# First pair's weight operands stored to DRAM for the second pair, and seven-product down projection in the second pair's layer two

## The chip, the cores and the metric

The kernel runs on one core of a Trainium2 chip. The metric is the device time of one execution in microseconds, as the median of several runs. Engines: PE is TensorE (PEld its weight loads), DVE is VectorE, ACT is ScalarE, POOL is GpSimd, SP is SyncE, which issues all DMAs here.

## The reference, cut to what matters

Four sequences of 512 rows with 512 features go through an attention block with two feed-forward networks, and then through three adapter layers with experts picked for each sequence (the "units" of the kernel, 3 x 4 = 12).

```
attn_out = softmax(x Wq (x Wk)^T / sqrt(512)) (x Wv) Wp + bp
cms      = gelu(attn_out @ cW1 + cb1) @ cW2 + cb2 + one_hot(code)        # layer one:  512 -> 2048 -> 512
modifier = gelu(concat[attn_out, cms] @ mW1 + mb1) @ mW2 + mb2           # layer two: 1024 -> 2048 -> 512
y0       = clip(x + cms + modifier, 0, 1)
for layer in 1..3:   y = layernorm(y + gelu(y @ Wd[e] + bd[e]) @ Wu[e] + bu[e]) * gamma[e] + beta[e]
```

## The kernel before

**Arithmetic.** All data is 32 bit. Each operand of a product is split in a high part (a cast to fp32r, on ACT) and the rest (operand minus high part, on DVE). A product is three matmuls, high x high, high x low, low x high; `mm3` at line 557 issues them, so nearly all matmuls have that line.

**Feed-forward part.** The sequences go in two pairs. Each pair has 8 chunks: four of layer one, four of layer two (`chunk_of`; chunks 0 to 7 are the first pair, 8 to 15 the second). A chunk takes two hidden tile pairs ("quads", q = 0, 1). Its **up** part computes the hidden block of both row halves and both sequences with seven block products (P1, P6, P7, P5, P2, P4, P3) in place of eight, six matmuls of 128 x 512 for each part of a product: 14 steps in layer one, 28 in layer two (`up_quad`). P1's bank is copied to u_t by ACT (`copy_first`, line 930), and P2 goes on in the same bank; DVE combines the products (v_t, w_t, g), ACT does the gelu. A weight operand of a product is 128 x 256: raw pieces of 512 KB arrive in `rawp`, DVE makes four sums of blocks in `asum`, ACT casts an operand into one of six `ring` slots (`weight_hi`, line 906) and DVE subtracts (`weight_lo`, line 1224), AHEAD = 5 steps before its use. Both pairs do that with the same weights.

The **down** part has eight steps d of 12 matmuls (`down_chunk`), 96 in all: four row tiles by two sequences by four output tiles. It needs split rows of the down weight (`w_hl`, from `wraw`; `down_weight_hi`, `down_weight_lo` at line 1285) and splits of g (`g_hl`, three slots; `g_hi`, `g_lo`). During steps 0 to 4 ACT and DVE also make the first five ring operands of the next chunk. DVE adds the eight banks to `res` after it.

**SP's queue** is in order and written out by hand. At the start it loads the inputs, waits for the expert numbers and then runs 36 pieces of the adapter weights through three `prep` slots: load (line 419), cast on ACT (`piece_hi`), rest on POOL (`piece_lo`, line 1545), store (line 415). ACT has `piece_hi` between its copies out of PSUM and ahead of the exps (line 822). In the feed-forward part SP issues `raw_piece` (430), `down_weights` (435), seven 1 MB stores of the second pair's operands in chunks 1 to 3, their loads `next_a_operand` (441) in chunk 7, x of the first pair (`xs`, 2 MB) there, y0 of the first pair (`y0_spill`, 2 MB) in chunk 9 and its split (`y0_split`, 4 MB) in chunk 11. In the last chunk it loads yT, x of the second pair, y0, the first adapter weights (wd, wu), the up biases and twelve `unit_columns` of 5 KB (502).

**Hand-over to the adapters.** TensorE transposes y0 of sequence 0 (`y0_to_rows(0)`, line 721), does the down product of unit 0, transposes y0 of sequence 1, and goes on unit by unit. DVE first clips y0 of both sequences of the second pair (`second_pair_y0`, line 1362), then adds the bias to the rows (`y0_rows`, line 1442), and later sums z and takes its statistics (`z_stats`).

## Time and profile before

| | us |
|---|---|
| median of 3 runs | 1193.47 (1193.29 to 1194.72) |
| the profiled execution's own time | 1194.04 |
| its span in the trace | 1192.2 |
| PE busy | 1178.7 (99%) |
| DVE busy | 790.8 (66%) |
| ACT busy | 569.3 (48%) |
| POOL busy | 162.5 (14%) |
| DMA, mean busy share of 16 engines | 34.7%, 145.82 MB |

Busy times say how full an engine is. The chain that ended last says on which engine the time was spent that led to the end. In the timeline the bracket behind a row gives the idle time of the engine before it and who ended it. For DMAs two things count: when SP issues them, and when they land.

### The profile page before, as it was taken

The numbers are of one execution on the slowest core, as the hardware profiler recorded it, in microseconds if no ns is written. First come the engines' busy times: TensorE is split into PE (matmuls) and PEld (weight loads), VectorE is DVE, ScalarE is ACT, GpSimd is POOL, SyncE is SP. The second block draws the span as 40 slices with busy tenths as digits, with TensorE's granted clock in tenths as the row PEclk, the third lists the DMA queues.
The fourth block names the chain that finished last, engine by engine and source line by source line (L and its number), as shares of the span: only waits on it lengthen the run. The fifth ranks groups of instructions, "written<-read, shape, count | busy, mean of one in ns | idle before, by whom it ended". The sixth has DMA issues, their size and how long they took to land.

```text
span 1192.2 us, 15272 instructions
## 1 busy us (share of the span) xinstructions
PE 1178.7 (99%) x5328; PEld 973.9 (82%) x5328; DVE 790.8 (66%) x1460; ACT 569.3 (48%) x1068; POOL 162.5 (14%) x145
## 2 busy tenths in 40 slices
PE   9999999999999999999999999999999999999997
PEld 7888878888888788888888888878888888788886
DVE  6344486776678756565667686696656565877885
ACT  5434353563544534342435643554343434357886
POOL 1332230000000000000000000000000000349981
PEclk9999999999999999999999999999999999999999
DMA  6764452124320302020561321411111118746644
GB/s 226 273 216 161 164 175 94 54 60 153 124 96 28 107 13 95 10 98 8 194 258 53 124 62 45 178 53 53 54 53 54 54 36 326 223 142 224 218 167 169
DMA packets 50610, 145.82 MB, mean 122 GB/s; under 512 B 6356, under 2 KB 6356, under 8 KB 46310
## 3 DMA queue, kind: packets, MB, share of 16 engines
q1 hardware_dynamic: 50534, 144.84, 34.7%
q8 instruction: 43, 0.70, 0.2%
q14 instruction: 33, 0.27, 0.1%
HBM read 108.11 MB, written 36.71 MB: 121 GB/s over the span
## 4 chain that ended last, share of the span: by engine, by line
PE 92%; DVE 5%; issue 1%; DMA 1%; ACT 1%; POOL 0%; POOLq 0%; DVEq 0%; SPq 0%; ACTq 0%
PE psum L557 89%; PE psum L777 2%; DVE c_op L1334 1%; DVE res L1362 1%; DVE ring L1224 1%; DVE res L1307 1%; PE psum L608 0%; PE psum L591 0%; PE psum L721 0%; PE psum L604 0%; DMA wqk_raw<-wqk_dram 0%; DVE sm L1477 0%; DMA prep<-wdu_dram 0%; DVE z L1471 0%; DVE c_t L1319 0%
## 5 line engine op out<-in xcount | busy, mean ns | idle before, releaser
L557 PE MATMUL psum<-g_hl,w_hl 128*128 128x512 f32 x1536 | 351.3, 389 | 0.4 <-DVE w_hl L1285 0.4
L557 PEld LDWEIGHTS psum<-g_hl,w_hl 128*128 128x128 f32 x1536 | 288.1, 188 | 61.0 <-DVE w_hl L1285 0.8
L557 PE MATMUL psum<-a_op,ring 128*128 128x512 f32 x1344 | 316.7, 389 | 0.7 <-DVE w_t L1266 0.7
L557 PEld LDWEIGHTS psum<-a_op,ring 128*128 128x128 f32 x1344 | 252.1, 188 | 54.0 <-DVE w_t L1266 1.5
L906 ACT CAST ring<-asum 128x256 fp32r<-128x256 f32 x192 | 77.2, 404 | 210.5 <-PE psum L557 160.0
L557 PE MATMUL psum<-c_op,ring 128*128 128x512 f32 x672 | 163.9, 391 | 0.8 <-DVE c_op L1334 0.6
L557 PEld LDWEIGHTS psum<-c_op,ring 128*128 128x128 f32 x672 | 125.5, 188 | 29.4 <-DVE c_op L1334 3.6
L1292 DVE TENSOR_TENSOR g_hl<-g,g_hl 128x512 fp32r<-128x512 f32 x128 | 88.2, 689 | 67.9 <-ACT g_hl L946 66.5
L1553 POOL TENSOR_TENSOR yT<-res,yT 128x512 fp32r<-128x512 f32 x8 | 11.7, 1488 | 846.3 <-ACT yT L1044 846.3
L1224 DVE TENSOR_TENSOR ring<-asum,ring 128x256 fp32r<-128x256 f32 x192 | 80.5, 421 | 56.1 <-ACT ring L906 54.9
L946 ACT CAST g_hl<-g 128x512 fp32r<-128x512 f32 x128 | 78.3, 618 | 77.5 <-PE psum L557 77.5
L923 ACT ACTIVATE g<-g,sm 128x512 f32<-128x512 f32 x96 | 69.5, 724 | 78.8 <-DVE g L1272 31.5
L1224 DVE TENSOR_TENSOR ring<-rawp,ring 128x256 fp32r<-128x256 f32 x144 | 60.7, 423 | 62.8 <-ACT ring L906 61.6
L906 ACT CAST ring<-rawp 128x256 fp32r<-128x256 f32 x144 | 57.6, 404 | 55.3 <-PE psum L557 55.3
L1307 DVE TENSOR_TENSOR res<-psum,res 128x512 f32<-128x512 f32 x96 | 64.8, 691 | 20.2 <-PE psum L557 18.6
L557 PE MATMUL psum<-wu,h_hl 128*128 128x512 f32 x288 | 68.4, 393 | 0.0
L557 PE MATMUL psum<-yT,wd 128*128 128x512 f32 x288 | 67.8, 391 | 0.0
L1545 POOL TENSOR_TENSOR prep<-prep 128x512 f32<-128x512 f32 x36 | 50.2, 1401 | 126.4 <-ACT prep L817 126.4
L557 PEld LDWEIGHTS psum<-yT,wd 128*128 128x128 f32 x288 | 53.8, 188 | 11.1
L557 PEld LDWEIGHTS psum<-wu,h_hl 128*128 128x128 f32 x288 | 53.3, 188 | 10.7
L1285 DVE TENSOR_TENSOR w_hl<-wraw,w_hl 128x512 fp32r<-128x512 f32 x64 | 44.1, 689 | 20.3 <-ACT w_hl L937 19.3
L557 PE MATMUL psum<-vp_w,xT 128*128 128x512 f32 x192 | 45.3, 391 | 0.0
(128 smaller groups left out, 1352.7 us busy)
## 6 DMA issues: line engine op xcount, KB each, us to landing
rawp<-up_w_dram SPq DMA_DIRECT2D x48, 512.0 KB, 3.6
wdu_split<-prep SPq DMA_DIRECT2D x36, 512.0 KB, 2.9
wraw<-dn_w_dram SPq DMA_DIRECT2D x64, 256.0 KB, 3.3
wd<-wdu_split SPq DMA_DIRECT2D x12, 1024.0 KB, 9.1
wu<-wdu_split SPq DMA_DIRECT2D x12, 1024.0 KB, 5.4
prep<-wdu_dram SPq DMA_DIRECT2D x36, 256.0 KB, 3.3
second_pair_operands<-c_op SPq DMA_DIRECT2D x7, 1024.0 KB, 6.3
a_op<-second_pair_operands SPq DMA_DIRECT2D x7, 1024.0 KB, 11.7
```

The source lines that it names most:

```text
L557: ins = nc.tensor.matmul(ps, lw(el), rw(er), start=first and i == 0, stop=last and i == 2, skip_group_check=skip)
L777: ins = nc.tensor.transpose(tr_bank(u, d)[:, i * P:(i + 1) * P], z[u % 3][:, i, d * P:(d + 1) * P], ident[:, :])
L906: nc.scalar.copy(ring[n % RING][:, 0, :], aop_src(n)).then_inc(aop_hi, 1)
L923: nc.scalar.activation(dst, src, ACT.Gelu, bias=(cb1, mb1)[l][:, t:t + 1]).then_inc(gelu_done, 1)
L946: nc.scalar.copy(g_hl[t % GHL][:, 0, :], g[:, q, 2 * row + seq, :]).then_inc(g_hi_done, 1)
L1224: nc.vector.tensor_tensor(ring[n % RING][:, 1, :], aop_src(n), f(ring[n % RING][:, 0, :]), ALU.subtract).then_inc(aop_lo, 1)
L1285: nc.vector.tensor_tensor(w_hl[t % 2][:, 1, :], wraw[t % 2][:, :], f(w_hl[t % 2][:, 0, :]), ALU.subtract).then_inc(w_lo_done, 1)
L1292: nc.vector.tensor_tensor(g_hl[t % GHL][:, 1, :], g[:, q, 2 * row + seq, :], f(g_hl[t % GHL][:, 0, :]), ALU.subtract).then_inc(g_lo_done, 1)
L1307: nc.vector.tensor_tensor(dst, bank[4 * seq + m], dst, ALU.add).then_inc(d_evac, 1)
L1334: nc.vector.tensor_tensor(c_ops[i][:, 1, :, :], src, f(c_ops[i][:, 0, :, :]), ALU.subtract).then_inc(op_lo[2 + p], 1)
L1362: nc.vector.tensor_scalar(res[:, 2 + seq, m, :], res[:, 2 + seq, m, :], 0.0, 1.0, ALU.max, ALU.min).then_inc(y0_done, 1)
L1545: nc.gpsimd.tensor_tensor(prep[i][:, 1, :], prep[i][:, 1, :], prep[i][:, 0, :], ALU.subtract).then_inc(p_lo, 1)
```

## The change

The first pair stores each finished ring operand (high and low part, 256 KB) to DRAM (`store_operand`), 168 of them. The second pair doesn't split up weights: SP loads each operand into its ring slot as soon as the operand six steps earlier is used (`load_operand`). In layer one of the second pair (chunks 8 to 11), ACT and DVE use the freed time to split 56 operands of the layer-two down weight into four `stage` slots, from where they are stored too; the cast for slot n waits for the store of n - 4. In layer two of the second pair (chunks 12 to 15), the down part uses seven block products: 14 steps of six matmuls, with 14 splits of g or of sums of g (`g_sum`, `g_op_hi`, `g_op_lo`) and seven adds of two banks (`down_product_add`). The transfers of x, y0 and y0_split are cut into pieces of 512 KB and put between the ring loads of chunks 8, 9 and 10. The twelve `unit_columns` go to the start, ahead of the prep pieces. In the last chunk and behind it the loads are put between and behind the ring loads, and DVE adds x and clips after `y0_rows(0)` and `y0_rows(1)`.

```diff
+CS = NCHUNK + NCHUNK // 2
+LOADED = AOP
+PREPARED = AOP + PROD * QL
+DOWN_STEPS = (tuple((i, 0) for i in (P1, P6, P7, P5)) + tuple((i, 1) for i in (P1, P6, P7, P5))
+              + tuple((i, q) for i in (P2, P4, P3) for q in range(QC)))
+CSTEP = len(DOWN_STEPS)
+STG = 4
+DG = 8
...
+            for u in range(LAYERS * B):
+                unit_columns(u)
+
             def bsum_store():
...
+            def store_operand(n):
+
+                sp.wait_ge(aop_lo, n + 1)
+                src = f(aop_dst(n)[:, :, :].rearrange("p e n -> p (e n)"))
+                if n < LOADED:
+                    sp.dma_start(up_ops[n], src).then_inc(s_wst[n % RING], 16)
+                else:
+                    sp.dma_start(down_ops[n - LOADED], src).then_inc(s_dst[n % STG], 16)
+
+            def load_operand(r):
+                sp.wait_ge(aop_used, r - RING + 1)
...
+                sp.dma_start(f(ring[r % RING][:, :, :].rearrange("p e n -> p (e n)")),
+                             (up_ops, down_ops)[down][i]).then_inc(s_ring[r % RING], 16)
...
+            for r in range(LOADED, LOADED + RING):
+                load_operand(r)
+            for i in (P2, P4, P3):
+                next_a_operand(NCHUNK - 1, i)
...
+            for ci in range(NCHUNK, CS):
+                first, ops = aop_at(ci, 0), QC * PROD
+                down_weights(4 * ci)
+                down_weights(4 * ci + 1)
+                for k in range(-STG, ops):
+                    if k >= 0:
+                        load_operand(first + RING + k)
+                    if k + STG < ops:
+                        store_operand(first + STG + k)
+                        pieces_after(first + STG + k)
+                    if ci == NCHUNK and 4 <= k < 8:
+                        x_piece(k - 4)
+                    if ci == NCHUNK + 1 and 0 <= k < 4:
+                        y0_piece(k)
+                    if ci == NCHUNK + 2 and 1 <= k < 9:
+                        y0_split_piece(k - 1)
+                    if k == ops - 3:
+                        down_weights(4 * ci + 2)
+                down_weights(4 * ci + 3)
...
+            last_up = aop_at(NCH - 1, 1)
+            for r in range(PREPARED + RING, TOTAL):
+                load_operand(r)
+                if r in (last_up + RING + 3, last_up + RING + 5):
+                    split_rows(0, (r - last_up - RING - 3) // 2)
+                if r == last_up + RING + 7:
+                    unit_down(0)
+                if r in (last_up + RING + 13, last_up + RING + 15):
+                    seq = (r - last_up - RING - 13) // 2
+                    sp.wait_ge(aop_used, last_up + LAYER_STEPS[1].index((P3, 0)) + 1)
+                    sp.dma_start(xs[1][:, seq, :, :], xin[2 + seq]).then_inc(s_xs[1], 16)
+                if r == last_up + RING + 16:
+                    for b in range(B):
+                        sp.dma_start(bup0[:, b, :], bup_all[bass.ds(ex[b], 1)].to_broadcast([P, V])).then_inc(t_bup0, 16)
+            sp.wait_ge(s_spill, 16 * 4)
+            sp.wait_ge(aop_used, dop_at(NCH - 1, 7) + 1)
             sp.dma_start(res[:, 0, :, :], y0_dram[:, 0]).then_inc(s_y0in[0], 16)
...
             unit_up(0)
+            unit_down(1)
+            for e in range(2):
+                split_rows(1, e)
+            sp.wait_ge(aop_used, dop_at(NCH - 1, 8) + 1)
+            sp.wait_ge(f_done, 3)
             sp.dma_start(res[:, 1, :, :], y0_dram[:, 1]).then_inc(s_y0in[1], 16)
-            unit_down(1)
             unit_up(1)
...
+            def down_products(ci):
+                for step, (prod, q) in enumerate(DOWN_STEPS):
+                    r, t = dop_at(ci, step), CSTEP * (ci - CS) + step
+                    if q == 0:
+                        down_step_bank_free(ci, prod)
+                    pe.wait_ge(s_ring[r % RING], 16 * ((r - LOADED) // RING + 1))
+                    pe.wait_ge(dg_lo, t + 1)
+                    for m in range(2):
+                        ins = mm3(bank[ADD_BANK[ADDS.index(prod)] + m], lambda e: ring[r % RING][:, e, m * P:(m + 1) * P],
+                                  lambda e: dg[t % DG][:, e, :], prod <= P5 and q == 0, q == QC - 1, skip=prod > P5)
+                    ins.then_inc(aop_used, 1)
...
-                nc.scalar.copy(ring[n % RING][:, 0, :], aop_src(n)).then_inc(aop_hi, 1)
+                if n < LOADED:
+                    if n >= RING:
+                        act.wait_ge(aop_used, n - RING + 1)
+                        act.wait_ge(s_wst[n % RING], 16 * (n // RING))
+                elif n < LOADED + STG:
+                    act.wait_ge(aop_used, LOADED)
+                else:
+                    act.wait_ge(s_dst[n % STG], 16 * ((n - LOADED) // STG))
+                nc.scalar.copy(aop_dst(n)[:, 0, :], aop_src(n)).then_inc(aop_hi, 1)
...
-            second_pair_y0(0)
-            second_pair_y0(1)
+            down_product_add(NCH - 1, 6)
             y0_rows(0)
...
                 if s == 0:
+                    x_add(0)
+                    second_pair_y0(0)
                     h_lo(0, 0)
                     h_lo(0, 1)
                     y0_rows(1)
+                    x_add(1)
+                    second_pair_y0(1)
```

## Rows read from the trace of the kernel before

**Rows 1.** The page, busy times and the chain that ended last.
```profile
PE 1178.7 (99%) x5328; PEld 973.9 (82%) x5328; DVE 790.8 (66%) x1460; ACT 569.3 (48%) x1068; POOL 162.5 (14%) x145
...
PE 92%; DVE 5%; issue 1%; DMA 1%; ACT 1%; POOL 0%; POOLq 0%; DVEq 0%; SPq 0%; ACTq 0%
```

**Rows 2.** Timeline of PE (start, duration, us), down 7, up 8, down 8.
```profile
594.40 21.92 PE L557 MATMUL psum<-g_hl,w_hl 128*128 128x512 f32 x96
616.16 19.20 PE L557 MATMUL psum<-a_op,ring 128*128 128x512 f32 x84
635.20 21.92 PE L557 MATMUL psum<-g_hl,w_hl 128*128 128x512 f32 x96
```

**Rows 3.** Timeline of PE, chunk 12: up begins, one gap, down begins.
```profile
779.36 5.60 PE L557 MATMUL psum<-a_op,ring 128*128 128x512 f32 x24
...
792.34 1.67 PE L557 MATMUL psum<-c_op,ring 128*128 128x512 f32 x6 [0.28 <-DVE c_op L1334]
...
819.41 21.92 PE L557 MATMUL psum<-g_hl,w_hl 128*128 128x512 f32 x96
```

**Rows 4.** Line 502, two column loads; duration ns, first and last start us.
```profile
L502 SPq DMA_DIRECT2D unit_columns<-pp_dram x2: 332/332/333, 1014.6 to 1015.2; - x2
```

**Rows 5.** Timelines of SP, ACT and POOL in the first phase of pieces.
```profile
18.70 0.83 SPq L419 DMA_DIRECT2D prep<-wdu_dram  x2
...
26.61 0.44 SPq L419 DMA_DIRECT2D prep<-wdu_dram  x1
...
21.98 0.62 ACT L817 CAST prep<-prep 128x512 fp32r<-128x512 f32 x1
...
30.91 1.29 POOL L1545 TENSOR_TENSOR prep<-prep 128x512 f32<-128x512 f32 x1 [3.94 <-ACT prep L817]
...
47.08 0.62 ACT L817 CAST prep<-prep 128x512 fp32r<-128x512 f32 x1 [2.11 <-DMA prep<-wdu_dram]
47.60 0.68 ACT L822 ACTIVATE probs<-psum,sm 128x512 f32<-128x512 f32 x1
```

**Rows 6.** Timelines of PE and DVE, attention of the first sequence.
```profile
49.95 8.33 PE L557 MATMUL psum<-vp_w,xT 128*128 128x512 f32 x36
...
62.63 10.72 PE L557 MATMUL psum<-pT,v_n 128*128 128x512 f32 x46
...
63.91 0.68 DVE L1109 TENSOR_TENSOR v_n<-psum,v_n 128x512 fp32r<-128x512 f32 x1
```

**Rows 7.** Windows: us, busy of PE, PEld, DVE, ACT, POOL, PEclk, DMA share, GB/s.
```profile
585.00:590.00 5.00, 5.00 (x24) 4.14 (x23) 3.77 (x7) 1.82 (x4) 0.00 (x0) 1.00 0.96 333
600.00:605.00 5.00, 5.00 (x23) 4.14 (x23) 3.00 (x6) 2.38 (x5) 0.00 (x0) 1.00 1.02 426
1058.00:1062.00 4.00, 4.00 (x21) 3.30 (x19) 3.99 (x10) 0.69 (x1) 2.25 (x3) 1.00 1.05 404
```

**Rows 8.** A lone 256 KB load (line 435, at 630.1); 256 KB stores at the end.
```profile
DMA to landing us min/median/max: 2.5/2.5/2.5
...
out_dram<-res SPq DMA_DIRECT2D x8, 256.0 KB, 2.2
```

**Rows 9.** Groups of instructions: busy us, mean ns, idle before.
```profile
L906 ACT CAST ring<-asum 128x256 fp32r<-128x256 f32 x192 | 77.2, 404 | 210.5 <-PE psum L557 160.0 <-DVE asum L1239 48.6 <-DVE asum L1242 2.0
...
L930 ACT COPY u_t<-psum 128x512 f32<-128x512 f32 x32 | 18.7, 586 | 0.0
...
L1357 DVE TENSOR_TENSOR res<-res,xs 128x2048 f32<-128x2048 f32 x2 | 4.6, 2289 | 1.1 <-DMA xs<-x_dram 1.1
```

**Rows 10.** Timeline of SP in chunk 7.
```profile
585.61 2.07 SPq L441 DMA_DIRECT2D a_op<-second_pair_operands  x4
```

**Rows 11.** Timeline of DVE, down part of chunk 7, last down weight.
```profile
606.79 0.69 DVE L1285 TENSOR_TENSOR w_hl<-wraw,w_hl 128x512 fp32r<-128x512 f32 x1
```

**Rows 12.** Timeline of PE, transposes of y0 of sequences 0 and 1.
```profile
1020.70 1.91 PE L721 MATMUL psum<-ident,res 128*128 128x128 f32 x16
...
1029.41 2.36 PE L721 MATMUL psum<-ident,res 128*128 128x128 f32 x16 [1.32 <-DVE res L1442]
```

More of the change, by code:

```diff
@@ L1022, in _ @@
                                 g_hi(ci, {1: 0, 2: 1, 4: 2}[at_])
+                if ci >= CS:
+                    gelu(ci, 1, C12)
+                    for d in range(CSTEP):
+                        for step in G_OP_DOWN.get(d, ()):
+                            g_op_hi(ci, step)
+                    continue
                 for d in range(DSTEP):
@@ L1095, in _ @@
                 if s == 0:
+                    y0_hi(2)
                     y0_hi(3)
@@ L1404, in _ @@
                                 g_lo(ci, {1: 0, 2: 1, 4: 2}[at_])
+                if ci >= CS:
+                    combine_12(ci, 1)
+                    for d in range(CSTEP):
+                        for k in G_SUM_DOWN.get(d, ()):
+                            g_sum(ci, *k)
+                        if d in ADD_AT:
+                            down_product_add(ci, ADD_AT[d])
+                        for step in G_OP_DOWN.get(d, ()):
+                            g_op_lo(ci, step)
+                        if ci == NCH - 1 and d in (9, 11, 13):
+                            first_sum_add((9, 11, 13).index(d))
+                    continue
                 for d in range(DSTEP):
```

308 lines of the change are left out of this document (230 added, 78 removed).

## The prediction

> **What bounds the kernel now.** I read the page first. Its busy times and the chain that ended last [rows 1] say the same: TensorE is busy for 1178.7 of 1192.2 us and carries 92% of the chain. So a matmul that goes away is worth its full time, and every wait that TensorE gets is paid in full. Next I read TensorE's timeline. A chunk of the feed-forward part is 84 matmuls up and 96 down in layer one, back to back: 616.16 to 635.20 is 19.04 us, and 594.40 to 616.16 is 21.76 us [rows 2]. Both give 0.2267 us for each matmul. One up product of six matmuls is a step of 1.36 us. The only gaps in the feed-forward part of the second pair stand at the start of its layer two, where the operands of that layer come late from DVE [rows 3].
>
> The second thing to read is the DMA queue. All DMAs are issued by SP in order, and they run through one hardware queue. Before the change that queue is mostly idle in the second pair, and the change fills it.
>
> **What the change removes.** In chunks 12 to 15 the down part goes from 96 to 84 matmuls: 4 x 12 x 0.2267 = **-10.9 us**. In the same chunks DVE and ACT no longer split weights. Up part 12 lasts 819.41 - 779.36 = 40.05 us, and its 168 matmuls would be 38.08 us, so 1.97 us is stall, waiting for c_op on DVE [rows 3]. DVE's queue there holds the weight work between the c_op jobs. When it goes, the c_op jobs move up, by more than the 0.3 us gaps: **-1.9 us** (between -1.97 and 0). The 14 operand splits per chunk that come instead of 8 are spread over a DVE that has lost its weight work. I walked its queue through one down part (sums, splits, PSUM adds at about 0.69 us each) and each product finds its operand about 1 us early or more; I cost this at nothing, and at 1 us per chunk if that cover fails.
>
> **Columns at the start.** The twelve loads of unit_columns move from the last chunk, where they cost TensorE nothing, to a place ahead of the prep pieces in SP's queue. At an idle queue they are issued 0.55 us apart: two of them start at 1014.6 and 1015.2 [rows 4]. (Behind a full queue, earlier in that series, they took up to twice that; I take the row of the idle queue, since at 18.7 us little is in flight.) So the first prep load goes from 18.70 to 18.7 + 12 x 0.55 = 25.3 us. It lands 3.3 us later, as it does now (18.70 to 21.98), at 28.6. The cast takes 0.62, POOL 1.3, and then SP stores it and issues the third load, at 31.0 instead of 26.61 [rows 5]: 4.4 us late. From there on the pieces have no slack. ACT waits for the DMA before the last piece at 47.08 as well [rows 5], and ACT has the pieces ahead of the exps. So the first exp ends at 52.7 instead of 48.3 [rows 5]. TensorE wants its bank at 49.95 and waits 2.8 us [rows 6]. In the next round a piece stands ahead of the pT and v_n copies: the last v_n half ends at 64.59, and the k = 3 matmul of the product that began at 62.63 wants it at 62.63 + 9 x 0.227 = 64.67 [rows 6]. That leaves 0.1 us, so nearly the whole 4.4 us arrives: **+4.3 us**. Bounds: 2.5 us if an issue costs 0.4 us, the cost of a prep load's issue, and 9 us if it costs 0.94.
>
> **Staging in the second pair's layer one.** I count in units of 256 KB. Saturated, the queue moved 426 GB/s with 8 KB rows and 404 with 2 KB rows [rows 7]; I take 415, which is 0.63 us for a unit. One unit alone lands in 2.5 us as a load and in 2.2 us as a store [rows 8], so a load has 1.9 us and a store 1.6 us on top of its transfer. In each step SP issues the load for the operand six products on, and the store of the stage operand four on; stage operand j+4 can't be cast before the store of operand j has landed, and ACT is blocked there with copy_first and the gelus queued behind it. Two units per 1.36 us step is 1.26 us: it just fits. What is put between them doesn't.
> - Chunk 10, y0_split as eight pieces of 2 units. From the end of product 0 until the load of operand 13 lands: 8 loads + 7 stores + 6 pieces x 2 + a raw piece of 2 = 29 units, 18.3 + 1.9 = 20.2 us. TensorE wants it after 12 x 1.36 = 16.3 us. Stall 3.9 us.
> - Chunk 9, y0 as four pieces. Until store 9: 6 + 6 + 8 + 2 = 22 units, 13.9 + 1.6 = 15.5 us, then the cast and copy_first behind it, 0.40 + 0.59 [rows 9]: 16.5 us. The P2 product of the second quad wants u_t after 13.6 us. Stall 2.9 us.
> - Chunk 8, x as four pieces: 23 units until load 13, 14.5 + 1.9 = 16.4 against 16.3 us. Stall 0.1 us.
> - Down part of chunk 7. The next-pair operands are issued from about 587.5 on (now 585.61 [rows 10]; the last stores of layer two come first). Then 28 units of a_op, three of down weights, six ring loads and the first stage store, 38 x 0.63 = 23.9 us, plus 1.0 for the first stretch, which ran at 333 GB/s [rows 7], plus 1.6: 614.0 us. That store is behind down weight 33, which waits for w_lo at 607.48 [rows 11], so issue isn't the limit. ACT is blocked on it with g_hi(7) behind: 0.40 + 0.62 + 0.69 gives 615.7 us, and step 7 begins at 594.40 + 7 x 2.72 = 613.4. Stall 2.3 us.
>
> Sum **+9.2 us**. Bounds: 3 us, if each of the four waits is met by 1.5 us of slack that I don't see; 13 us if the rate is 404 GB/s and each wait meets another 0.6 us.
>
> In the first pair one unit per step is stored (the queue is less than half full), each store is issued some five steps before its slot is wanted, and I cost it at nothing. If SP were blocked there in front of a store, ACT would feel it; the DMA waits that it passes (down weights, pieces) are all satisfied by then.
>
> **Chunk 15 and the end.** The queue there gets yT, wd, x and up-bias loads among the ring loads. Counted from the start of the down part, the load behind x and the four biases needs 5 + 8 + 4 = 17 units, 10.7 + 0.3 left over + 1.9 = 12.9 us, and it is wanted after 9 x 1.36 = 12.2: **+0.7 us** (0 to 2). Then res[:, 1], y0 of the second sequence, is now the last of 45 units: 28.4 + 0.3 + 1.9 = 30.6 us. The transposes of y0_to_rows(1) want it 19.04 + 0.7 + (1029.41 - 1.32 - 1020.70 = 7.39) = 27.1 us after the same point [rows 12]. That is 3.5 us of wait where 1.32 us of another wait (DVE clips before y0_rows) is now: **+2.2 us** (-1.3 to 4.5). DVE now does x_add(1), 2.3 us [rows 9], and four clips between y0_rows(1) and z_stats(0), in which the next transposes wait for z: **+0.8 us** (0 to 3).
>
> **The sum** is -10.9 - 1.9 + 4.3 + 9.2 + 0.7 + 2.2 + 0.8 = +4.4 us. It is made against the profiled execution, 1194.04 us (1.8 us around its span), which lies 0.6 us above the median of 1193.47. So 1198.4 on the profile's scale, **1197.9 us** as a median.
>
> **A rule weighed.** The stretch at 600 us moved 426 GB/s from DRAM into SBUF for 5 us, with the DMA engines' share at 1.0 [rows 7]. The Trainium skill, "DMA: Bandwidth & Descriptors", section "Specifications", gives about 358 GB/s as the HBM limit of a core, and the same page says that this side binds for transfers between HBM and SBUF. By 358 a unit would be 0.73 us, and the same counts would add about 3 us in chunk 10, 2 each in chunks 8 and 9, 4 in chunk 7 and 5 at the end: an estimate of some 1214 us. The trace disagrees for loads; no row has loads and stores mixed at saturation.
>
> **Rivals.**
> - *The queue is hidden.* The staging waits don't reach TensorE, because SP itself is held back (stores wait for aop_lo) and ACT's jobs have more room than I give them. For: the ring is six deep, and ACT isn't the engine that bounds the kernel now. Against: the byte counts leave nothing in chunk 10. Then -10.9 - 1.9 + 4.3 + 0.7 + 2.2 + 0.8 = -4.8: 1188.7 us, and 1187 with the cheap start. It decides the sign: faster as soon as staging costs under 4.8 us. Chance 0.27.
> - *Half of it.* The start costs 2.5 us and the staging about 5 us: -10.9 - 1.9 + 2.5 + 5 + 3.7 = -1.6, 1191.9 us, and with what lies around it (1191.1 to 1195.9) no change that can be told. Chance 0.15.
> - *The mixed queue is slow.* Loads and stores together run at the 333 GB/s that the stretch at 585 us had with a share of 0.96 [rows 7]: 0.79 us a unit. Then chunk 10 costs 8.5, chunk 9 6.4, chunk 8 3.8 and chunk 7 7.4 us, and the wait at the end is 10.7 us: about 1222 us. The page of the rule above is on this side. Chance 0.08.
> - *The products don't fit the down part.* DVE adds seven pairs of banks and makes 14 splits; if they come 1 us late in each of four chunks, 1202 us. In the range of my forecast.
>
> **How the numbers follow.** My forecast, slower by 2.4 to 12 us, has 0.50. A measurement of this kernel can tell about 0.2% (2.4 us) from no change. Faster 0.27, same 0.15, slower 0.50 + 0.08 = 0.58. The range leaves out about one in ten at each end: below the cheapest version of the hidden queue (1187) and above my upper bounds taken together for start and staging without the slow mixed queue (1208). My forecast's own range is 1196 to 1206.
>
> **What would show it.** In the profile of the changed kernel the twelve column loads stand before the first prep load, which goes out near 25 us; TensorE has a wait on ACT or DVE near 50 us and one near 65 us. Eight pieces of y0_split put a wait for the DMA of ring in the up part of chunk 10, some 4 us; chunks 8 to 10 last longer than 40.8 us, chunks 12 to 15 last 57.1 us. TensorE's transposes near the end wait for the DMA of res. If chunks 8 to 10 last 40.8 us, the queue count is wrong, and the kernel is faster.

## The result, and the profile after

The changed kernel takes **1237.2 us** (median of 4 runs, 1234.7 to 1239.8) against 1194.1 in the same session, a ratio of 1.036 with the interval 1.0335 to 1.0384: slower by some 43 us. I had forecast 1197.9 with a range from 1187 to 1208. The sign was right, the size was not. The profiled execution took 1237.19 us and has a span of 1235.4, 43.2 us more than before. Here are the lines of its page that answer to [rows 1]:

```profile
span 1235.4 us, 15542 instructions
...
PE 1185.1 (96%) x5280; PEld 972.4 (79%) x5280; DVE 761.7 (62%) x1351; ACT 531.2 (43%) x964; POOL 162.6 (13%) x146
...
PE 77%; DMA 9%; DVE 7%; SPq 2%; ACT 2%; issue 2%; POOL 1%; POOLq 0%; DVEq 0%; ACTq 0%
PE psum L710 75%; DMA down_operands<-stage 4%; DMA prep<-wdu_dram 2%; PE psum L970 2%; DMA ring<-down_operands 1%; DMA experts<-experts_dram 1%; DVE g_hl L1521 1%; POOL prep L1851 1%; DMA res<-y_spill 1%; DVE c_op L1561 1%; DVE a_op L1376 0%; SPq L481 0%; ACT prep L1010 0%; PE psum L744 0%; DVE xs L1568 0%
```

Two things stand in these lines. TensorE has 48 matmuls fewer and is still busy for 6.4 us longer. By count it should be busy for 1178.7 - 10.9 = 1167.8 us, so its matmuls ran 17.3 us slower. And its idle time has gone from 13.5 to 50.3 us. The chain, once TensorE with a rest, now goes through stage stores (4%) and g_hl. The waits of TensorE say who ended that idle time (us in total, times, longest):

```profile
PE psum L710 <- DVE g_hl L1521: 12.6, 3, 5.9
PE psum L710 <- DMA ring<-up_operands: 7.8, 7, 1.9
PE psum L710 <- DMA ring<-down_operands: 5.8, 2, 4.6
PE psum L710 <- ACT u_t L1132: 5.2, 3, 2.5
...
PE psum L710 <- ACT probs L1015: 3.0, 1, 3.0
```

TensorE's timeline (start, duration, [idle before <- releaser]) has them in place. These are waits of chunks 7 to 10, then the start of chunk 15, its two longest waits and the first transposes behind it:

```profile
599.97 19.20 PE L710 MATMUL psum<-g_hl,w_hl 128*128 128x512 f32 x84
625.07 5.18 PE L710 MATMUL psum<-g_hl,w_hl 128*128 128x512 f32 x12 [5.89 <-DVE g_hl L1521]
...
674.37 4.49 PE L710 MATMUL psum<-g_hl,w_hl 128*128 128x512 f32 x12 [2.38 <-DVE g_hl L1521]
...
697.18 2.18 PE L710 MATMUL psum<-a_op,ring 128*128 128x512 f32 x6 [1.89 <-DMA ring<-up_operands]
...
730.01 5.49 PE L710 MATMUL psum<-g_hl,w_hl 128*128 128x512 f32 x12 [4.30 <-DVE g_hl L1521]
...
756.88 1.65 PE L710 MATMUL psum<-a_op,ring 128*128 128x512 f32 x6 [2.49 <-ACT u_t L1132]
...
996.25 5.60 PE L710 MATMUL psum<-a_op,ring 128*128 128x512 f32 x24
...
1036.51 12.51 PE L710 MATMUL psum<-dg,ring 128*128 128x512 f32 x54 [1.19 <-DMA ring<-down_operands]
1053.64 9.99 PE L710 MATMUL psum<-dg,ring 128*128 128x512 f32 x30 [4.63 <-DMA ring<-down_operands]
1063.47 1.91 PE L914 MATMUL psum<-ident,res 128*128 128x128 f32 x16
```

Look at the durations too. The 12 matmuls at 625.07 took 5.0 us until the next part began, where 12 x 0.2267 is 2.7. The windows (us, busy of PE, PEld, DVE, ACT, POOL, PEclk, DMA share, GB/s) show why:

```profile
625.00:630.00 5.00, 4.93 (x12) 3.97 (x13) 4.38 (x8) 0.01 (x1) 0.00 (x0) 0.53 0.01 2
635.00:640.00 5.00, 5.00 (x24) 4.14 (x23) 1.95 (x5) 0.81 (x2) 0.00 (x0) 1.00 0.92 288
...
730.00:735.00 5.00, 4.99 (x12) 3.93 (x13) 4.33 (x7) 0.00 (x0) 0.00 (x0) 0.50 0.00 0
...
1045.00:1050.00 5.00, 4.01 (x18) 3.00 (x16) 5.00 (x9) 0.62 (x1) 0.00 (x0) 1.00 0.95 201
1055.00:1060.00 5.00, 5.00 (x13) 3.84 (x12) 2.42 (x3) 0.00 (x0) 0.00 (x0) 0.52 1.02 406
```

Behind the waits of 5.9, 4.3 and 4.6 us the granted clock is 0.50 to 0.53, the lower of TensorE's two levels (1.2 GHz). So such a wait costs more than its length.

From the starts of the parts in this timeline the whole difference can be laid out, against 0.2267 us for a matmul. The start is 216.26 against 210.65 us before. Chunk 15 is 67.2 us from 996.25 to 1063.47, where its 252 matmuls are 57.1. The row behind it is the stretch from the end of the last down part to the last of the transposes of y0, 38.05 us from 1063.47 against 36.86 from 1020.70 [rows 12], and the last one is all that follows, 133.9 us against 134.6:

| part | forecast | measured |
|---|---|---|
| start, up to the first a_op matmul | +4.3 | +5.6 |
| chunk 7, down (30.1 us for 21.8) | +2.3 | +8.4 |
| chunk 8, up / down (22.5 / 26.1) | +0.1 / 0 | +3.5 / +4.3 |
| chunk 9, up / down (27.8 / 28.8) | +2.9 / 0 | +8.8 / +7.0 |
| chunk 10, up / down (26.9 / 21.8) | +3.9 / 0 | +7.9 / 0 |
| chunk 11, up | 0 | +0.1 |
| chunk 12's stalls | -1.9 | -2.0 |
| 48 matmuls | -10.9 | -10.9 |
| chunk 15 | +0.7 | +10.1 |
| rows and first units behind it | +3.0 | +1.2 |
| the rest of the adapters | 0 | -0.8 |
| sum | +4.4 | +43.2 |

### The profile page after: what moved, and what is told of

Its sections match the earlier page's. It is cut to its first block, busy times and chain, and to the rows that moved or that the text cites. A ratio compares the mean times of both kernels' runs of the same rounds, so it can differ in the third digit from the quotient of the medians.

```text
span 1235.4 us, 15542 instructions
## 1 busy us (share of the span) xinstructions
PE 1185.1 (96%) x5280; PEld 972.4 (79%) x5280; DVE 761.7 (62%) x1351; ACT 531.2 (43%) x964; POOL 162.6 (13%) x146
## 4 chain that ended last, share of the span: by engine, by line
PE 77%; DMA 9%; DVE 7%; SPq 2%; ACT 2%; issue 2%; POOL 1%; POOLq 0%; DVEq 0%; ACTq 0%
PE psum L710 75%; DMA down_operands<-stage 4%; DMA prep<-wdu_dram 2%; PE psum L970 2%; DMA ring<-down_operands 1%; DMA experts<-experts_dram 1%; DVE g_hl L1521 1%; POOL prep L1851 1%; DMA res<-y_spill 1%; DVE c_op L1561 1%; DVE a_op L1376 0%; SPq L481 0%; ACT prep L1010 0%; PE psum L744 0%; DVE xs L1568 0%
## 5 line engine op out<-in xcount | busy, mean ns | idle before, releaser
L710 PE MATMUL psum<-g_hl,w_hl 128*128 128x512 f32 x1152 | 270.8, 396 | 13.0 <-DVE g_hl L1521 12.6
L710 PEld LDWEIGHTS psum<-g_hl,w_hl 128*128 128x128 f32 x1152 | 220.1, 192 | 61.4 <-DVE g_hl L1521 13.8
L710 PEld LDWEIGHTS psum<-c_op,ring 128*128 128x128 f32 x672 | 125.8, 188 | 27.8 <-DVE c_op L1561 1.8
L1521 DVE TENSOR_TENSOR g_hl<-g,g_hl 128x512 fp32r<-128x512 f32 x96 | 66.1, 688 | 49.5 <-ACT g_hl L1148 48.4
L710 PE MATMUL psum<-dg,ring 128*128 128x512 f32 x336 | 80.1, 400 | 5.8 <-DMA ring<-down_operands 5.8
L1105 ACT CAST ring<-asum 128x256 fp32r<-128x256 f32 x96 | 38.5, 404 | 104.1 <-PE psum L710 76.0
L710 PEld LDWEIGHTS psum<-dg,ring 128*128 128x128 f32 x336 | 65.0, 194 | 20.4 <-DMA ring<-down_operands 5.1
L1148 ACT CAST g_hl<-g 128x512 fp32r<-128x512 f32 x96 | 58.4, 617 | 45.0 <-PE psum L710 45.0
L1132 ACT COPY u_t<-psum 128x512 f32<-128x512 f32 x32 | 18.7, 584 | 88.8 <-PE psum L710 88.7
L1453 DVE TENSOR_TENSOR ring<-asum,ring 128x256 fp32r<-128x256 f32 x96 | 40.1, 420 | 26.4 <-ACT ring L1105 25.8
L1534 DVE TENSOR_TENSOR res<-psum,res 128x512 f32<-128x512 f32 x72 | 47.4, 687 | 13.1 <-PE psum L710 13.0
L1453 DVE TENSOR_TENSOR ring<-rawp,ring 128x256 fp32r<-128x256 f32 x72 | 30.3, 422 | 32.0 <-ACT ring L1105 31.4
```

The lines of the kernel that those rows point to most:

```text
L710: ins = nc.tensor.matmul(ps, lw(el), rw(er), start=first and i == 0, stop=last and i == 2, skip_group_check=skip)
L1105: nc.scalar.copy(aop_dst(n)[:, 0, :], aop_src(n)).then_inc(aop_hi, 1)
L1132: nc.scalar.copy(u_t[:, :], bank[4 * q + BANK_OF[P1]]).then_inc(u_done, 1)
L1148: nc.scalar.copy(g_hl[t % GHL][:, 0, :], g[:, q, 2 * row + seq, :]).then_inc(g_hi_done, 1)
L1453: nc.vector.tensor_tensor(aop_dst(n)[:, 1, :], aop_src(n), f(aop_dst(n)[:, 0, :]), ALU.subtract).then_inc(aop_lo, 1)
L1521: nc.vector.tensor_tensor(g_hl[t % GHL][:, 1, :], g[:, q, 2 * row + seq, :], f(g_hl[t % GHL][:, 0, :]), ALU.subtract).then_inc(g_lo_done, 1)
```

## Why the down parts stall

The g_hl waits, in parts that I had costed at nothing apart from chunk 7's, are the largest of TensorE's waits in total, 12.6 us. Down part 8 begins at 652.62. Rows of DVE, SP and ACT in it:

```profile
657.75 0.43 DVE L1453 TENSOR_TENSOR stage<-rawp,stage 128x256 fp32r<-128x256 f32 x1 [0.42 <-ACT stage L1105]
...
663.51 5.41 SPq L543 DMA_DIRECT2D wraw<-dn_w_dram  x2
668.96 2.05 SPq L526 DMA_DIRECT2D down_operands<-stage  x4
...
672.25 0.40 ACT L1105 CAST stage<-rawp 128x256 fp32r<-128x256 f32 x1 [7.35 <-DMA down_operands<-stage]
672.56 0.61 ACT L1148 CAST g_hl<-g 128x512 fp32r<-128x512 f32 x1
```

The first stage operand is complete at 658.2. SP stores it at 668.96, since the two down weights stand ahead of it in SP's order, and the second waits for DVE's last w_lo. The store lands 3.2 us later. ACT then makes the fifth staged operand, whose slot this was, and only then g_hl(7), whose buffer TensorE had freed at 652.62 + 5 x 2.72 = 666.2. There are four stage slots, and ACT and DVE work five products ahead. That is my theory of the down parts, **the order**: a cast one place too far ahead couples TensorE to a store that is issued late. The rival is **the queue**: the stores land late because the queue is full, whatever the order. In chunk 7 the queue has a case. The stage stores went out at 613.46 behind 28 units of a_op, and ACT was released at 623.36. In chunk 10 the same cast waits too:

```profile
779.02 0.41 ACT L1105 CAST stage<-rawp 128x256 fp32r<-128x256 f32 x1 [4.55 <-DMA down_operands<-stage]
```

There the last w_lo is done 13.1 us after the part's start (15.9 and 14.8 us in chunks 8 and 9), and g_hl(7) is ready 0.6 us before TensorE wants it. So it is a near miss, not a part without the chain.

## The experiments

The bracket is a 95% interval of the ratio.

| kernel | us | against the kernel before |
|---|---|---|
| the change | 1237.2 | 1.036 (1.0335 to 1.0384) |
| column loads late | 1229.0 | 1.0303 (1.0281 to 1.0326) |
| g_hi first | 1224.6 | 1.0261 (1.0240 to 1.0282) |
| one less ahead | 1216.2 | 1.0173 (1.0156 to 1.0191) |
| stage stores first | 1217.8 | 1.0189 (1.0167 to 1.0210) |
| and pieces moved | 1206.7 | 1.0111 (1.0094 to 1.0128) |
| and columns, up bias moved | 1201.0 | 1.0057 (1.0036 to 1.0078) |
| and store ahead of load | 1197.5 | 1.0021 (1.0008 to 1.0034) |
| and a lighter end | 1195.0 | 1.0003 (0.9993 to 1.0012) |
| and one less ahead, end in order | 1189.0 | 0.9957 (0.9943 to 0.9970) |
| before, 48 matmuls fewer | 1182.9 | 0.9908 (0.9891 to 0.9924) |

**The columns, put back behind the prep pieces.**

```diff
-            for u in range(LAYERS * B):
-                unit_columns(u)
-
             def bsum_store():
...
+            for u in range(LAYERS * B):
+                unit_columns(u)
             sp.wait_ge(op_lo[0], PROD)
```

> The changed kernel with one thing put back: the twelve unit_columns loads are issued behind the 72 prep loads and 72 stores instead of ahead of them. Theory (the start term is right in kind): TensorE's feed-forward part begins 5.6 us earlier, at 210.7 instead of 216.3 us, the V product begins at 49.95 instead of 52.90, and the whole is 5.6 us faster, 1231.6 us. Rival (the start's delay comes from elsewhere, or is taken up later by another wait): less than 2 us. Nothing else in the trace should move but by a shift.

1229.0 us. The gain by the medians is 8.2 us, of which 5.2 can be seen in the trace as the start; the intervals don't separate it from 5.6. (The prep loads and stores that the expectation counts as 72 each are 36 each.) The executions of these stalled kernels lie 4 to 7 us apart, so small steps between them are read from the places in the trace and not from the medians. The rows of the changed kernel, SP's and then TensorE's, followed by TensorE's first a_op row of this experiment:

```profile
18.93 7.13 SPq L481 DMA_DIRECT2D unit_columns<-pp_dram  x12
26.11 0.91 SPq L505 DMA_DIRECT2D prep<-wdu_dram  x2
...
52.90 10.04 PE L710 MATMUL psum<-vp_w,xT 128*128 128x512 f32 x36 [2.98 <-ACT probs L1015]
...
67.47 11.53 PE L710 MATMUL psum<-pT,v_n 128*128 128x512 f32 x48
...
216.26 6.05 PE L710 MATMUL psum<-a_op,ring 128*128 128x512 f32 x26
```

```profile
211.02 11.27 PE L709 MATMUL psum<-a_op,ring 128*128 128x512 f32 x49
```

The g_hl waits stayed in their places and nearly in their length (5.15, 2.50 and 3.86 us for 5.89, 2.38 and 4.30), so the start's delay is one of its own.

**g_hl(7) ahead of the fifth staged operand.** The same edit is made on DVE.

```diff
-                    if d < AHEAD and ci + 1 < CS:
+                    late = ci + 1 >= NCHUNK
+                    if d < AHEAD - late and ci + 1 < CS:
                         weight_hi(aop_at(ci + 1, 0) + d)
+                    if late and d == AHEAD and ci + 1 < CS:
+                        weight_hi(aop_at(ci + 1, 0) + AHEAD - 1)
```

> The changed kernel, but in the down parts of chunks 7 to 10 ACT and DVE do the split of the next chunk's fifth staged weight operand behind the split of g_hl(7) instead of ahead of it; SP's order is untouched. Theory (TensorE waits for g_hl(7) because ACT is held at that operand's cast until a stage store has landed, and g_hi(7) is queued behind): the waits on DVE g_hl before the eighth block of chunks 7, 8 and 9 (5.89, 2.38 and 4.30 us) go, and with each the slow stretch behind it; chunk 7's down part goes from 30.1 to about 22 us, chunk 8's from 26.1 to 22, chunk 9's from 28.8 to 22: 15 to 19 us less, about 1219 us. Rival (the next up part then waits for the late operand's own store instead, so the wait is only moved): the down parts are 21.8 us, but the up parts of chunks 8 to 10 grow by what is gained, and the whole is within 4 us of 1237.

1224.6 us: 12.6 less, between theory and rival. All three g_hl waits are gone, but the place behind them has its own. TensorE's rows in up part 8:

```profile
624.09 7.10 PE L710 MATMUL psum<-a_op,ring 128*128 128x512 f32 x30 [2.57 <-DVE res L1537]
...
642.40 1.66 PE L710 MATMUL psum<-a_op,ring 128*128 128x512 f32 x6 [2.35 <-ACT u_t L1132]
```

DVE is now held at the fifth operand with down_add (L1537) queued behind it, which empties the banks for the next part. So it isn't enough to take g_hl out from behind the blocked cast, since whatever comes behind it then is blocked in its place.

**Stage stores first.**

```diff
-                down_weights(4 * ci)
-                down_weights(4 * ci + 1)
-                for k in range(-STG, ops):
+                for k in range(STG):
+                    store_operand(first + k)
+                    if k % 2:
+                        down_weights(4 * ci + k // 2)
+                if ci == NCHUNK:
+                    for i in (P2, P4, P3):
+                        next_a_operand(NCHUNK - 1, i)
+                for k in range(ops):
```

> The changed kernel, but SP issues the first four stage stores of chunks 8 to 11 between the down weights (store, store, weight, store, store, weight) instead of behind both weights, and ahead of the loads of a_op P2, P4 and P3 in chunk 7. Theory (the stores are late because they are issued late, at 16.3 us into the down part of chunk 8): they are issued up to 6 us earlier, land before ACT wants the slot, and the waits on g_hl in the down parts of chunks 7 to 9 go: 15 to 19 us less, about 1219 us, nearly the same gain as from changing the order on ACT. Rival (the queue itself is full, and a store issued earlier lands no earlier): chunk 7 keeps its 5.9 us wait and chunk 9 its 4.3; the gain is under 5 us, from chunk 8 alone.

1217.8 us, 19.4 less, as the theory has it. The g_hl waits of chunks 7, 8 and 9 are all gone, and chunk 7's down part runs without a gap:

```profile
600.49 21.92 PE L712 MATMUL psum<-g_hl,w_hl 128*128 128x512 f32 x96
622.25 15.12 PE L712 MATMUL psum<-a_op,ring 128*128 128x512 f32 x66
```

In the changed kernel the queue was nearly idle before the stores of chunks 8 and 9 (a DMA share of 0.09 from 660 to 665 us and of 0.14 from 715 to 721), so the order on SP alone held them back. In chunk 7 the edit also takes 12 units of a_op from ahead of the stores. Order and queue aren't separated there.

**One number: four ahead instead of five.** SP's order is left as it was.

```diff
+def ahead(ci):
+
+    return AHEAD if ci < NCHUNK else AHEAD - 1
...
-                    if d < AHEAD and ci + 1 < CS:
+                    if d < ahead(ci + 1) and ci + 1 < CS:
                         weight_hi(aop_at(ci + 1, 0) + d)
```

> The changed kernel with one number changed: in chunks 8 to 11 ACT and DVE make a staged weight operand four products ahead of its place instead of five (there are four stage slots). SP's order is that of the changed kernel. Theory (five ahead with four slots is what couples TensorE to the landing of a store: operand j+4's cast waits for store j while g_hi and copy_first stand behind it): no cast in a down part has to wait for a stage store, so the g_hl waits of chunks 7, 8 and 9 go with their slow stretches (19.6 us over the nominal 21.8 us of these parts), and the u_t waits of the up parts shrink as well: 20 to 25 us less, 1212 to 1217 us. Rival (the slot's wait only moves to the first products of the next up part, as it did when the split of g_hl was put ahead): 10 to 13 us less, 1224 to 1227.

1216.2 us, 21 less. ACT's rows and then TensorE's, for chunk 7:

```profile
615.33 0.62 ACT L1153 CAST g_hl<-g 128x512 fp32r<-128x512 f32 x1 [1.58 <-PE psum L715]
624.38 0.41 ACT L1110 CAST stage<-rawp 128x256 fp32r<-128x256 f32 x1 [8.44 <-DMA down_operands<-stage]
...
601.47 21.92 PE L715 MATMUL psum<-g_hl,w_hl 128*128 128x512 f32 x96
623.23 15.12 PE L715 MATMUL psum<-a_op,ring 128*128 128x512 f32 x66
```

The store lands as late as in the changed kernel, at 624.4, and no one is waiting: g_hl(7) is made at 615.3, when TensorE frees its buffer. This decides for the order. The late store is harmless until something that TensorE needs is queued behind it. The u_t waits went too, but 10.3 us of waits on ring<-up_operands stayed in up parts, and 4.0 us on w_t.

**The one-time pieces out of the up parts**, on top of stage stores first.

```diff
-                    if ci == NCHUNK and 4 <= k < 8:
-                        x_piece(k - 4)
-                    if ci == NCHUNK + 1 and 0 <= k < 4:
-                        y0_piece(k)
-                    if ci == NCHUNK + 2 and 1 <= k < 9:
-                        y0_split_piece(k - 1)
...
+                if ci == NCHUNK:
+                    for k in range(4):
+                        x_piece(k)
+                if ci == NCHUNK + 3:
+                    for k in range(8):
+                        y0_split_piece(k)
```

> The stores-first kernel, and in it the one-time traffic of the second pair's layer one is taken out of the up parts: the x pieces go out at the start of chunk 8's down part, the y0 pieces after the first stage stores of chunk 10, the eight y0_split pieces at the start of chunk 11's down part, and the a_op loads P1, P6, P7, P5 inside chunk 7's store loop; DVE's y0_add jobs move to steps 2 to 5 of chunk 8's down part. Theory (the up parts of chunks 8, 9 and 10 stall because these pieces stand between ring loads and stage stores that have 1.36 us each): the waits on u_t and ring there (2.2, 6.0 and 5.6 us, with the half-clock stretches behind them some 20 us) go, up parts of 19.1 us as in chunk 11, and the whole is about 1199 us. Rival (a store takes so long to land, 3 to 5 us, that ACT is held whatever stands between): the u_t waits stay in chunks 8 to 10, the gain is under 8 us, above 1210 us.

1206.7 us: 11.1 less, where I expected 19. The waits on ring<-up_operands in chunks 8 to 10 are all gone, so the pieces were their cause. Waits of 0.5 to 1.1 us on u_t and 0.8 on w_t stayed, 5.2 us with all of them, so a part of the rival was true. In the two profiled executions the up parts of chunks 8 to 11 lose 15.5 us (22.6 us above 19.04 each before, 7.1 after), more than the 11.1 of the medians; the rest of the difference isn't explained.

**Columns late and the up bias spread out**, on top of that.

```diff
-                if r == last_up + RING + 16:
-                    for b in range(B):
+                if r - last_up - RING in (8, 9, 10, 11):
+                    for b in (r - last_up - RING - 8,):
```

> The pieces-moved kernel with two more edits: the column loads behind the prep pieces, and the four up-bias loads of the last chunk one by one among ring loads 8 to 11 of the last quad instead of together behind load 16. Theory: the start gives back 5.6 us, and the wait of 4.6 us on ring with its slow stretch in the last down part shrinks to under 1.5 us, together some 10 us: 1189 us, below the kernel before. Rival (the bytes of the last chunk don't fit wherever they stand): the same wait shows up earlier, in the last up part or on yT at its end, and only the 5.6 us of the start are gained, 1193.5 us.

1201.0 us, 5.8 less: the start, and nothing from chunk 15. Its waits of 1.2 and 4.5 us on ring became three of 1.2, 1.3 and 1.8, and the wait on res behind it grew from 1.6 to 3.6 us. The rival held in this, though the wait went behind the chunk and not ahead of it: with this order and these bytes, what is moved off one load lands on another.

**Each store ahead of its step's load**, on top of that (chunks 8 to 11).

```diff
                 for k in range(ops):
-                    load_operand(first + RING + k)
                     if k + STG < ops:
                         store_operand(first + STG + k)
+                    load_operand(first + RING + k)
+                    if k + STG < ops:
                         pieces_after(first + STG + k)
```

> The all-moved kernel, and in chunks 8 to 11 each step issues its stage store ahead of its ring load instead of behind it. Theory (what is left in those up parts, waits of 0.6 to 0.9 us on u_t and of 0.8 us on w_t, 5.6 us in all, comes from stores that SP holds back behind a load that waits for TensorE, so that ACT's cast and copy_first behind it come a step late): a store goes out up to 1.36 us earlier, those waits go, and the kernel takes 5 us less, 1196 us. Rival (a store is issued as soon as DVE has made it anyway, and the rest is the landing of 3 to 4 us): the waits stay as they are, under 1 us of gain.

1197.5 us, 3.5 less. The u_t waits are gone, the three on w_t of 0.6 to 0.8 us stayed.

**A lighter end**, on top of that. In the code DG goes from 8 to 6, and x_add is called in chunks 13 and 14.

```diff
+                if ci == 4:
+                    for b in range(B):
+                        sp.dma_start(bup_rows[:, b, :], bup_all[bass.ds(ex[b], 1)].to_broadcast([P, V])).then_inc(s_bupd, 16)
...
+                if r == last_up + RING + 9:
+                    sp.wait_ge(s_bupd, 16 * B)
+                    sp.dma_start(bup0[:, :, :], bup_rows).then_inc(t_bup0, 16)
```

> The store-ahead kernel with less traffic in chunk 15: the four one-row up-bias loads are made once into DRAM rows in chunk 4 (DRAM to DRAM) and read at the end as one load of 4 units; x of the second pair comes in four pieces in chunks 12 to 14 and is added there by DVE, through two buffers for which the ring of down-part operands dg shrinks from eight to six. Theory (the last chunk loses 4.2 us of waits on ring and 3.6 on res, with slow stretches, because its queue holds some 10 to 12 us more than fits): 8 units of x and 4 us of the one-row loads less (9 us of queue) take those waits to under 2 us together: 8 to 10 us faster than the store-ahead kernel, about 1187 us, below the kernel before (1194). Rivals: six dg buffers are too few and TensorE waits on dg in each of the four down parts (1 us each or more); or the one-row reads weren't the cause and the waits stay, 1194 us.

1195.0 us, 2.4 less where I expected 8 to 10 (the two intervals overlap a little). No wait on dg appeared, so six buffers do. The ring waits of the last down part shrank to 2.0 us, but the wait for res grew:

```profile
PE psum L930 <- DMA res<-y_spill: 5.5, 1, 5.5
```

SP issues that load last, behind one wu, one wd and two yT loads, when DVE's last sum is done. The queue was a third idle from 1005 to 1015 us (a share of 0.69 and 0.61) and full from 1015 on.

**The end in the order of need**, and four ahead, on top of that.

```diff
+                if r in (last_up + RING + 19, last_up + RING + 21):
+                    split_rows(1, (r - last_up - RING - 19) // 2)
-                if r == last_up + RING + 9:
+                if r == last_up + RING + 16:
...
-            unit_up(0)
             unit_down(1)
-            for e in range(2):
-                split_rows(1, e)
+            unit_up(0)
```

> The lighter-end kernel with that same four-ahead rule, and with chunk 15's loads in the order of their need: yT of the second sequence among the last ring loads, the up-bias rows at ring load 16, and res[1] right behind one wd and one wu load instead of behind those and two yT loads. Theory (the 5.5 us wait on res<-y_spill in the lighter-end kernel is 8 units of yT ahead of it in a full queue, while the queue was a quarter to a third idle from 1000 to 1015 us): that wait goes to under 1 us, and the 0.8 us waits on w_t in chunks 8 to 10 go too: 6 to 8 us less than 1195.0, about 1188 us, below the kernel before (1194.0) by 0.5%. Rival (bytes moved earlier make the ring loads late by as much): waits on ring in the last down part grow by 3 us or more, and it stays within 0.2% of the kernel before.

**1189.0 us** (1188.4 to 1190.2), 6.0 less and 0.4% below the kernel before. The 5.5 us wait shrank to 0.5, but the load of y0 of sequence 0 now comes 2.6 us late; the w_t waits are gone. The main waits of TensorE in it that the kernel before doesn't have:

```profile
PE psum L935 <- DMA res<-y_spill: 3.1, 2, 2.6
...
PE psum L731 <- DMA ring<-up_operands: 1.6, 2, 1.1
...
PE psum L731 <- DMA ring<-down_operands: 1.2, 1, 1.2
PE psum L731 <- DVE g_hl L1542: 0.9, 1, 0.9
```

What it gains is 5.1 of the 12.8 us that the idea is worth (10.9 of matmuls, 1.9 of chunk 12's stalls); most of the rest is in these rows.

**What the matmuls are worth**, on the kernel before. It leaves out one of the three terms in steps 1, 3 and 5 of the last four down parts.

```diff
+                            short=ci >= 3 * NCHUNK // 2 and d in (1, 3, 5)).then_inc(d_used, 1)
```

> The kernel before with 12 of the 96 matmuls left out of the down parts of chunks 12 to 15 (one of the three terms of steps 1, 3 and 5 is not computed), nothing else changed. Theory (what the products remove is worth its full time, 48 x 0.2267 us): 10.9 us faster, 1183.0 us. Rival (DVE's or ACT's splits become what TensorE waits for once the down part is 19 us long): new waits on g_hl or w_hl in chunks 12 to 15 and a gain under 6 us.

1182.9 us, 11.6 less (9 to 13 by the interval), and no wait on g_hl or w_hl that wasn't there before. The term of 10.9 us was right.

**TensorE's clock behind a wait**, on the kernel before.

```diff
+                    if q == 1 and pos == 0 and ci in PROBES:
+                        pe.wait_ge(s_probe, sorted(PROBES).index(ci) + 1)
```

> The kernel before, with eight waits put into TensorE's order, one ahead of the second quad of chunks 0, 1, 2, 3, 8, 9, 10 and 11, each ended by GpSimd after 1, 3, 6, 9, 13, 18, 26 and 40 small fills (idle of about 0.5 to 8 us). Theory (an idle of some 2 us or more costs its own length and then 4 to 5 us at half clock, about 2.3 us more): the chunks with a wait under 1 us are longer by the wait alone, those with a wait over 2 us by the wait and 2 to 2.5 us, with a granted clock near 0.5 for a few us behind it. Rival (the slow stretches in the changed kernel come from something else, the DMA traffic or the matmuls' own operands): each chunk is longer by exactly its wait, and the granted clock stays at 1.0 behind all eight.

Eight waits of 0.47 to 6.57 us, each followed by the 42 matmuls of a quad. Four of them:

```profile
633.31 9.80 PE L560 MATMUL psum<-a_op,ring 128*128 128x512 f32 x42 [2.35 <-POOL sm L1564]
...
677.52 12.64 PE L560 MATMUL psum<-a_op,ring 128*128 128x512 f32 x42 [3.13 <-POOL sm L1564]
...
725.82 12.37 PE L560 MATMUL psum<-a_op,ring 128*128 128x512 f32 x42 [4.38 <-POOL sm L1564]
...
776.04 11.23 PE L560 MATMUL psum<-a_op,ring 128*128 128x512 f32 x42 [6.57 <-POOL sm L1564]
```

Behind the waits up to 2.35 us the quad takes 9.80 us (9.68 without a wait). Behind those of 3.13, 4.38 and 6.57 us it takes 2.8, 2.6 and 1.4 us more. The granted clock is 0.50 just behind all three; it is still 0.74 from 682 to 685 us behind the first, and at 1.00 from 780 us on behind the last. So the slow stretches do come from waiting, and the longest wait didn't cost most. The Trainium skill, "TensorE: Matmul & The Clock Gate", section "HAM oscillation — how this bites in real kernels", tells of the same with DMA waits, behind each of which the matmuls start at the slower clock. The trace agrees, with the 0.50 behind these three. In the changed kernel the waits of 2.38 us at 674.37 and of 2.98 at 52.90 had slow stretches behind them as well (1.6 and 1.7 us), so the length of one wait doesn't settle it.

**The queue alone**, behind the last output of the kernel before.

```diff
+            for group in ((load,), (store,), (load, store), (rows_of_one,), (store, load)):
+                for i in range(8):
+                    for job in group:
+                        job(i)
+                sp.wait_ge(s_b, moved[0])
```

> The kernel before, and behind its last output store the chip only moves 256 KB units of 2 KB rows, each group waited for: 8 loads; 8 stores; 8 loads and 8 stores alternating; 8 loads that give one DRAM row to all 128 partitions; 8 and 8 again, store first; one load, one store, one of the one-row loads. Theory of the prediction: 0.63 us a unit in every group (loads 5 + 1.9 us, stores 5 + 1.6, mixed 10.1 + 1.9), a lone load 2.5 and a lone store 2.2 us. Rival that the changed kernel suggests: a unit of the mixed group takes 0.73 to 0.8 us (13 to 15 us for 16), a lone store over 3 us, and a one-row load 1.2 us (9.6 + 2 us for 8), since the stretch of the up-bias loads moved 201 GB/s.

SP's rows. Each group starts when the one before it has landed, so the starts give the times:

```profile
1191.27 3.67 SPq L554 DMA_DIRECT2D res<-dn_w_dram  x8
1200.12 4.46 SPq L558 DMA_DIRECT2D traffic<-res  x8
1206.94 0.33 SPq L554 DMA_DIRECT2D res<-dn_w_dram  x1
...
1220.15 6.58 SPq L562 DMA_DIRECT2D res<-bup_dram  x8
1234.94 0.33 SPq L558 DMA_DIRECT2D traffic<-res  x1
...
1250.02 0.33 SPq L558 DMA_DIRECT2D traffic<-res  x1
1252.03 0.34 SPq L562 DMA_DIRECT2D res<-bup_dram  x1
```

Eight loads take 8.9 us, eight stores 6.8, the mixed 16 units 13.2, and eight loads of one row each 14.8. The lone store takes 2.0 us, so it isn't the store as such that is slow. With 2 us for the landing of the first unit the mixed unit is 11.2 / 15 = 0.75 us against my 0.63, and the one-row unit is 12.8 / 7 = 1.8 us, nearly three times as much. In the second mixed group the queue reached 402 GB/s from 1240 to 1245 us. So the rate that I took is reached when the queue is full, but not on average in a burst that begins at an idle queue: 288 GB/s at a share of 0.92, in the window at 635 us above, is such a beginning.

## Why the prediction was wrong, by its own steps

- **The matmuls, and chunk 12's stalls**: right, by the shorter down parts, by up part 12 at 38.1 us from 824.89 (chunks 12 to 14 take 57.1 us each, as forecast), and by what the operand splits cost (nothing: no wait on dg in any run).
- **Columns at the start**: half right. TensorE waits 2.98 us at 52.90 where I had 2.8, behind a first prep load at 26.11 where I had 25.3. An issue took 7.13 / 12 = 0.59 us, not 0.55, and the row of the 0.55 didn't stand in an idle queue, as I had written: its DMA share from 1014 to 1016 us was 0.91. But the second wait, of some 1.5 us near 65 us, isn't there (no bracket in the row at 67.47). Nearly as much came from something that I had no term for: the 36 matmuls behind the first wait took 9.9 us for 8.2, at a granted clock of 0.50 from 53 to 55. That the total of 4.3 is near the 5.6 is in this part luck.
- **Staging**: the failed step, 9.2 forecast and 39.9 measured, of which 26.6 us are waits of TensorE and the rest is mostly slow matmuls behind them. It failed in three ways. First, I walked the ACT queue behind the stage stores in chunk 7 only. I wrote that the store "is behind down weight 33, which waits for w_lo", took that for harmless since the queue was the limit there, and never asked the same of chunks 8 and 9, where the queue was nearly empty and this order was the limit. Their down parts cost 11.3 us that have no term in my sum, and both stores first and one less ahead take them away. DVE has the y0_add and y0_lo jobs in just these two parts, ahead of the last w_lo; chunk 10 has neither, its w_lo comes 2 to 3 us earlier in the part, and it has no stall. No run takes these jobs out alone, so this cause is read from the rows. Second, I gave a store 1.6 us beyond its transfer, from the stores at the idle end of the kernel [rows 8]. That holds for a lone store (2.0 us), but the first four stage stores of a chunk took 3.2 to 3.8 us in chunks 8 and 10, 5.6 to 5.9 in chunk 9 and some 10 in chunk 7. Third, I counted units at 0.63 us from saturated windows [rows 7], where the mixed burst took 0.75. The last two bear on the up parts of chunks 8 to 10, 20.2 us where I had 6.9. The place was right, since the waits on ring went with the pieces and those on u_t with the earlier store; the size was not.
- **Each wait was priced at its length.** No row before has a long wait of TensorE in the feed-forward part, and I didn't ask what follows one. That is most of the 17.3 us of slower matmuls, of the 38.8 us that the sum was short. Not all of the 17.3 us is the clock: in the clock probe also a wait that left it at 1.00 made its chunk some 0.3 us longer than the wait and the matmuls, and the changed kernel has 19 waits up to the end of chunk 15 that the kernel before doesn't have, an estimated 5 us.
- **Chunk 15**: 0.7 forecast, 10.1 measured. The step was "four biases" as 4 units. They are one-row loads, and the window at 1045 us moved 201 GB/s at a share of 0.95. Nearly two thirds of the 10.1 us are waits, most of the rest is the slow stretch behind the longest.
- **The end**: 3.0 forecast, 1.2 measured. The wait for res[:, 1] is there, but 1.13 us long and not 3.5. Its load landed 35.5 us after the start of the down part where I had 30.6, and TensorE came for it 7.3 us later than I had, by the delays in chunk 15: a near cancellation that I didn't forecast. The wait of the next transposes for z was there too, 1.4 us where I had 0.8.
- **The rule weighed**: the trace disagrees with the 358 GB/s for loads and stores mixed as well, 402 GB/s in the queue's own run and 406 in the window at 1055 us. The 0.75 us of a unit in the mixed burst is near that rule's 0.73, but it is an average with a slow beginning, and not a limit. I had given the slow mixed queue 0.08, and of all my rivals its 1222 us came nearest to the result, but for another reason. It isn't shown by that.
- **The rivals**: "the queue is hidden" needed SP's holding back of stores to be harmless. It was what hurt.

The kernel at 1189.0 us keeps the products and the staging, and is 48 us faster than the change by the order of its work and by lighter traffic at its end. So neither the idea nor the count of its matmuls was at fault.

## What to carry to other kernels

When a step is staged through n slots, ask of every engine how far ahead it works, and what is queued behind the first instruction that needs a slot back. With one step more than there are slots, a store's landing is on the path, and the issuing engine's order decides how late that store is. Walk that chain in every stage that has it, since the stage with the full queue need not be the worst. And price a wait of TensorE of some 3 us or more at its length and 1.4 to 2.8 us more, on a path where TensorE is the bound; one of 2.4 us cost 1.6 us more here as well, and another of that length nothing.

## What the hardware showed that I had not expected

- A lone wait of TensorE of 3.1 us cost 2.8 us more than a short one, one of 6.6 us only 1.4, one of 2.35 us nothing.
- Reading one DRAM row of 2 KB into all 128 partitions takes 1.8 us for 256 KB where a load of distinct rows takes 0.6 [rows 7] to 1.0 (6.9 / 7, by the same count). Copied into DRAM once from DRAM to DRAM, in a quiet stretch, it costs nothing that the trace shows.
- A lone store landed faster than a lone load: 2.0 against 2.6 us in the queue's own run, 2.2 against 2.5 in [rows 8]. The Trainium skill, "DMA: Bandwidth & Descriptors", section "Latency and other measured facts", has DRAM as the slowest target for the receipt of a write. These two pairs don't show it.
